# A routed layer's expert results added straight into the output's rows by accumulating DMAs, instead of through a table in DRAM

## The reference, cut to what matters

```python
xn = _layernorm(x, axis=-1)
x = x + gnn(xn, ...) + mix(xn)          # the long part ahead; x is now the residual
...
t = _layernorm(x)
logits = t @ switch_w + switch_b
route_prob_max = jnp.max(softmax(logits), axis=-1)
routes = jnp.argmax(softmax(logits), axis=-1)
for e in range(8):
    y = gelu(t @ w1[e] + b1[e]) @ w2[e] + b2[e]      # 1024 -> 512 -> 1024
    out = jnp.where((routes == e)[:, None], y, out)
out = out * route_prob_max[:, None]
return x + out
```

## Time and profile of the kernel before

| What | Value |
|---|---|
| median of three timed runs | 651.61 us (647.75 to 652.52) |
| the profiled execution's own time | 647.44 us |
| its span, first to last instruction | 645.6 us |
| busy share of the span: TensorE | 88% |
| VectorE | 72% |
| ScalarE | 49% |
| GpSimd | 33% |
| mean granted TensorE clock | 0.961 |
| bytes moved by DMA | 102.69 MB |

### The profile page before, as it was taken

How to read it: one execution, slowest core, us unless ns; L and a number is a source line. 1 busy time by engine, 2 the same in 40 slices (tenths; PEclk the granted TensorE clock), 3 DMA queues, 4 the chain that set the end, 5 groups by cost and what they waited for, 6 DMA issues and landing times.

```text
span 645.6 us, 9295 instructions
## 1 busy us (share of the span) xinstructions
PE 568.3 (88%) x3090; PEld 519.5 (80%) x3090; DVE 462.3 (72%) x800; ACT 318.2 (49%) x474; POOL 213.3 (33%) x183
## 2 busy tenths in 40 slices
PE   2799999999999999999898898999898769888850
PEld 2799997889999999998887788999786657767640
DVE  6688887867446444645798977887879655999962
ACT  3445553310333333532655654766553345998950
POOL 5566765765399000600079661000001100000001
PEclk9899999999999999999999998999999959999995
DMA  8365558530633433563221432222662212999935
GB/s 303 128 205 162 176 174 246 119 92 0 222 122 119 161 130 130 150 225 99 69 94 65 131 128 71 93 94 73 229 196 75 88 32 95 334 412 411 412 93 200
DMA packets 32962, 102.69 MB, mean 159 GB/s; under 512 B 5376, under 2 KB 9536, under 8 KB 32928
## 3 DMA queue, kind: packets, MB, share of 16 engines
q1 hardware_dynamic: 27792, 90.02, 41.2%
q0 software_dynamic: 4992, 11.72, 5.9%
q10 hardware_dynamic: 144, 0.52, 0.3%
HBM read 96.65 MB, written 5.60 MB: 158 GB/s over the span
## 4 chain that ended last, share of the span: by engine, by line
PE 59%; DVE 22%; issue 6%; DMA 6%; ACT 5%; POOL 1%; DVEq 0%; POOLq 0%; ACTq 0%; SPq 0%
PE ps L1473 35%; DVE wsp L910 6%; PE ps L1487 4%; DVE big L910 4%; PE ps L1652 3%; DMA raw<-in_w_experts 3%; PE ps L1596 2%; PE ps L1742 2%; PE ps L1581 2%; PE ps L1543 2%; PE ps L1524 2%; PE ps L1606 2%; DVE stats L927 1%; PE ps L1616 1%; ACT wsp L601 1%
## 5 line engine op out<-in xcount | busy, mean ns | idle before, releaser
L1473 PE MATMUL ps<-big,wsp 128*128 128x384 f32 x1680 | 305.1, 340 | 9.7 <-DVE wsp L910 6.0
L1473 PEld LDWEIGHTS ps<-big,wsp 128*128 128x128 f32 x1680 | 295.8, 191 | 14.3 <-DVE wsp L910 5.6
L910 DVE TENSOR_TENSOR wsp<-raw,wsp 128x1024 fp32r<-128x1024 f32 x117 | 153.7, 1325 | 29.1 <-ACT wsp L601 23.2
L601 ACT ACTIVATE wsp<-raw 128x1024 fp32r<-128x1024 f32 x83 | 87.2, 1052 | 33.1 <-PE ps L1487 12.9
L463 POOL TENSOR_SCALAR rs<-mv 128x1 f32<-128x1 f32 x12 | 7.8, 647 | 184.1 <-DVE mv L1212 119.6
L507 POOL DMA_INDIRECT edge_table<-ef,eidx x48 | 55.8, 1163 | 32.1 <-DMA edge_table<-ef,eidx 19.2
L608 ACT ACTIVATE big<-ps,bias 128x384 f32 x24 | 14.0, 582 | 81.1 <-PE ps L1473 81.1
L921 DVE SCALAR_TENSOR_TENSOR big<-ps,bias,big 128x384 f32 x24 | 14.8, 618 | 51.5 <-ACT big L608 49.5
L910 DVE TENSOR_TENSOR big<-raw_x,big 128x1024 fp32r<-128x1024 f32 x36 | 42.1, 1219 | 0.3 <-ACT big L773 0.3
L570 POOL DMA_DIRECT2D slot_y<-maskb x8 | 4.3, 542 | 109.3 <-DVE maskb L1390 109.3
L773 ACT ACTIVATE wsp<-raw 128x1024 fp32r<-128x1024 f32 x34 | 34.5, 1048 | 6.6 <-DMA raw<-in_w_experts 4.0
(11 more groups left out here) (245 smaller groups left out, 864.4 us busy)
## 6 DMA issues: line engine op xcount, KB each, us to landing
raw<-in_w_stream SPq DMA_DIRECT2D x85, 512.0 KB, 3.4
raw<-in_w_experts SPq DMA_DIRECT2D x32, 512.0 KB, 6.0
raw_x<-in_w_experts SPq DMA_DIRECT2D x32, 512.0 KB, 6.5
rowbuf<-in_rowb POOLq DMA_DIRECT2D x6, 512.0 KB, 6.3
raw_x<-in_w_stream SPq DMA_DIRECT2D x4, 512.0 KB, 7.0
slot_y<-maskb POOLq DMA_DIRECT2D x8, 256.0 KB, 5.7
tok<-in_x SPq DMA_DIRECT2D x3, 512.0 KB, 4.1
edges_a<-in_src_rows SPq DMA_DIRECT2D x8, 192.0 KB
```

The costliest lines, as they stand in the source:

```text
L601: nc.scalar.activation(wsp[:, 0, slot, :], raw[:, slot, :], ACT.Copy).then_inc(w_hi, 1)
L910: return nc.vector.tensor_tensor(dst, value, hi.bitcast(F32), ALU.subtract)
L1473: ins = nc.tensor.matmul(ps[:, bank, 0:N], wsp[:, a, slot, k * P:(k + 1) * P], moving[:, b, k, :], start=(k == 0 and n == 0), stop=(k == K ...
```

## The change

The table in DRAM is gone, with the early zeros for it, the gather at the end, VectorE's last three sums and SyncE's stores of the output. Instead:

- GpSimd stores the three tiles of residual rows `tok` to the output as soon as VectorE has added the projection, and waits for them (`rows_out`).
- TensorE gets, for each slot, the number of the output's row and the probability of each of its 64 tokens: the one-hot matrices of the slot times a small matrix `tag` (row number less 512, probability high, probability low), 24 matmuls of 4 columns, right after the first `up_bias` and ahead of `up` of expert 1. VectorE reads them from PSUM (`meta`) into `row_of` and `prob_of`. A place without a token gets the row number 512.
- ScalarE multiplies the high rows by the probability as it copies them (`half_of_y`), VectorE multiplies the low rows and adds (`rows_of_y`, now a scalar_tensor_tensor).
- GpSimd sends each slot's rows with one indirect DMA that adds them in DRAM to the output's rows (`compute_op=ALU.add`). Rows with a number over 383 are left out by the bounds check. VectorE's next `rows_of_y` waits for this DMA as it did for the store.
- The last slot is taken in two halves of 512 columns: a new semaphore `y_half` is set when the first bank is done.
- VectorE's ten steps for the tokens' rows (nine now, as the cast to `posi` is gone) move from ahead of `got_low` to the start of `routes`, behind it. `pos_done`, for which TensorE waits ahead of `up` of expert 1, moves with them.

```diff
@@ constants
+NO_ROW = 512.0
+META = 4
@@ GpSimd
             pool.wait_ge(bd_added, NT)
-            then(nc.gpsimd.memset(rowbuf[0:SLOT, 0, :], 0.0))
-            for s in range(EXPERTS, SLOTS):
-                pool.dma_start(ys_dram[s * SLOT:(s + 1) * SLOT, :], rowbuf[0:SLOT, 0, :]).then_inc(zero_out, 16)
-            pool.wait_ge(zero_out, 16 * OVER)
...
+            pool.wait_ge(wo_sum, 2 * NT)
+            for t in range(NT):
+                pool.dma_start(out[t * P:(t + 1) * P, :], tok[:, t, :]).then_inc(rows_out, 16)
+            pool.wait_ge(rows_out, 16 * NT)
+
+            def add_rows(s):
+
+                pool.wait_ge(meta_done, 1 if s < EXPERTS else s - EXPERTS + 2)
+                pool.wait_ge(y_sum, s + (1 if s < EXPERTS - 1 else 2))
+                pool.indirect_dma_start(
+                    out=out, out_offset=bass.IndirectOffsetOnAxis(ap=row_of[:, s:s + 1], axis=0),
+                    in_=y_buf, in_offset=None, bounds_check=N - 1, oob_is_err=False,
+                    compute_op=ALU.add).then_inc(y_out, 16)
+
             for s in range(EXPERTS):
-                pool.wait_ge(y_sum, s + 1)
-                pool.dma_start(ys_dram[s * SLOT:(s + 1) * SLOT, :], y_buf).then_inc(y_out, 16)
+                add_rows(s)
+            pool.wait_ge(y_out, 16 * EXPERTS)
             over = pool.value_load(rowi[0:1, OVER:OVER + 1], min_val=0, max_val=OVER)
...
-            for t in range(NT):
-                pool.indirect_dma_start(
-                    out=x2[t], out_offset=None, in_=ys_dram,
-                    in_offset=bass.IndirectOffsetOnAxis(ap=posi[:, t:t + 1], axis=0)).then_inc(yg_in[t], 16)
@@ ScalarE
-            def low_rows_of_y(e):
+            def half_of_y(e, s):
 
                 act.wait_ge(y_ready, ys.add())
                 if ys.n > 1:
-                    act.wait_ge(y_sum, ys.n - 1)
-                nc.scalar.activation(y_tmp, whole(4 + 2 * (e % 2))[SLOT:P, :], ACT.Copy).then_inc(y_low, 1)
+                    act.wait_ge(y_sum, ys.n - 1 if s < EXPERTS else ys.n)
+                nc.scalar.activation(y_tmp, whole(4 + 2 * (e % 2))[0:SLOT, :], ACT.Identity,
+                                     scale=prob_of[:, s:s + 1]).then_inc(y_low, 1)
+
+            def last_half_of_y(e):
+
+                act.wait_ge(y_sum, e)
+                for h, ready in ((0, (y_half, 1)), (1, (y_ready, ys.add()))):
+                    act.wait_ge(*ready)
+                    nc.scalar.activation(y_tmp[:, h * HALF:(h + 1) * HALF], ps[0:SLOT, 4 + 2 * (e % 2) + h, :],
+                                         ACT.Identity, scale=prob_of[:, e:e + 1]).then_inc(y_low, 1)
@@ VectorE, constants
+            nc.vector.memset(tag[:].bitcast(F32), 0.0)
+            for t in range(NT):
+                nc.vector.tensor_scalar(rt[:, R_POS, NT + t:NT + t + 1], cst[:, C_EXP:C_EXP + 1], t * P - NO_ROW, None,
+                                        ALU.add)
@@ VectorE, ahead of the gather
             dve.wait_ge(lexp_done, NT)
+            nc.vector.tensor_copy(tag[:, :, 0], rt[:, R_POS, NT:2 * NT])
             then(nc.vector.reciprocal(rt[:, R_PROB, 0:NT], rt[:, R_SUM, 0:NT]))
+            then(nc.vector.tensor_copy(tag[:, :, 1], rt[:, R_PROB, 0:NT]))
+            lo(tag[:, :, 2], rt[:, R_PROB, 0:NT], tag[:, :, 1]).then_inc(tag_done, 1)
@@ VectorE, slots
-            def rows_of_y(e):
-
-                dve.wait_ge(y_low, ys.add())
-                if ys.n > 1:
-                    dve.wait_ge(y_out, 16 * (ys.n - 1))
-                nc.vector.tensor_tensor(y_buf, whole(4 + 2 * (e % 2))[0:SLOT, :], y_tmp, ALU.add).then_inc(y_sum, 1)
+            def meta(first, n):
+
+                metas = ps[0:SLOT, meta_bank(first), 0:SLOTS * META].rearrange("p (s c) -> p s c", c=META)
+                dve.wait_ge(meta_ready, 1 if first == 0 else first - EXPERTS + 2)
+                nc.vector.tensor_scalar(row_of[:, first:first + n], metas[:, first:first + n, 0], NO_ROW, None, ALU.add)
+                nc.vector.reduce_sum(prob_of[:, first:first + n], metas[:, first:first + n, 1:3], AX_X)\
+                    .then_inc(meta_done, 1)
+
+            def rows_of_y(e, s):
+
+                dve.wait_ge(y_low, ys.add() if s < EXPERTS else s + 2)
+                if s:
+                    dve.wait_ge(y_out, 16 * s)
+                nc.vector.scalar_tensor_tensor(out=y_buf, in0=whole(4 + 2 * (e % 2))[SLOT:P, :],
+                                               scalar=prob_of[:, s:s + 1], in1=y_tmp,
+                                               op0=ALU.mult, op1=ALU.add).then_inc(y_sum, 1)
+
+            def last_rows(e):
+
+                dve.wait_ge(y_out, 16 * e)
+                for h in range(2):
+                    dve.wait_ge(y_low, ys.add())
+                    cols = slice(h * HALF, (h + 1) * HALF)
+                    nc.vector.scalar_tensor_tensor(out=y_buf[:, cols], in0=ps[SLOT:P, 4 + 2 * (e % 2) + h, :],
+                                                   scalar=prob_of[:, e:e + 1], in1=y_tmp[:, cols],
+                                                   op0=ALU.mult, op1=ALU.add).then_inc(y_sum, 1)
@@ TensorE
+            def meta(s, one_hot):
+
+                for t in range(NT):
+                    ins = nc.tensor.matmul(ps[0:SLOT, meta_bank(s), s * META:(s + 1) * META], one_hot(t),
+                                           tag[:, t, :], start=(t == 0), stop=(t == NT - 1))
+                return ins
...
             up_bias(0, 0)
+            pe.wait_ge(tag_done, 1)
+            for s in range(EXPERTS):
+                ins = meta(s, lambda t: place[t][:, s * SLOT:(s + 1) * SLOT])
+            ins.then_inc(meta_ready, 1)
             pe.wait_ge(pos_done, 1)
```

More of the change, by code:

```diff
@@ L573, in _ @@
                 for s in range(EXPERTS, SLOTS):
-                    pool.wait_ge(y_sum, s + 1)
-                    pool.dma_start(ys_dram[s * SLOT:(s + 1) * SLOT, :], y_buf).then_inc(y_out, 16)
-            pool.wait_ge(pos_done, 1)
-            pool.wait_ge(y_out, 16 * EXPERTS)
-            over = pool.value_load(rowi[0:1, OVER:OVER + 1], min_val=0, max_val=OVER)
-            with pool.If(over > 0):
+                    add_rows(s)
                 pool.wait_ge(y_out, 16 * SLOTS)
-            for t in range(NT):
-                pool.indirect_dma_start(
-                    out=x2[t], out_offset=None, in_=ys_dram,
-                    in_offset=bass.IndirectOffsetOnAxis(ap=posi[:, t:t + 1], axis=0)).then_inc(yg_in[t], 16)
         @block.scalar
@@ L1338, in _ @@
-            end = cum[:, 3, 4:12]
-            first = rt[:, R_FIRST, 0:EXPERTS]
             def every_token(a):
                 return a.unsqueeze(1).to_broadcast([P, NT, EXPERTS])
-            then(nc.vector.scalar_tensor_tensor(out=first, in0=cum[:, 3, 3:11], scalar=float(SLOT),
-                                                in1=rt[:, R_TOTAL, 0:EXPERTS], op0=ALU.mult, op1=ALU.add))
-            then(nc.vector.scalar_tensor_tensor(out=tile3(R_RANK), in0=cnt.rearrange("p (t e) -> p t e", t=NT),
-                                                scalar=float(SLOT), in1=every_token(first),
-                                                op0=ALU.is_ge, op1=ALU.mult))
@@ L1398, in _ @@
             prep_x()
+            meta(0, EXPERTS)
             hidden(0)
@@ L1440, in _ @@
                         prep_x()
-                    rows_of_y(0)
-            for t in range(NT):
-                dve.wait_ge(yg_in[t], 16)
-                nc.vector.scalar_tensor_tensor(out=tok[:, t, :], in0=x2[t], scalar=rt[:, R_PROB, t:t + 1],
-                                               in1=tok[:, t, :], op0=ALU.mult, op1=ALU.add).then_inc(sum_done, 1)
+                    meta(EXPERTS + o, 1)
+                    rows_of_y(0, EXPERTS + o)
         @block.tensor
@@ L1838, in _ @@
                     pe.wait_ge(got_lo, KT + o + 1)
+                    meta(EXPERTS + o, lambda t: place_late[:, t, :]).then_inc(meta_ready, 1)
                     up(0, 0, 0)
```

62 lines of the change are left out of this document (36 added, 26 removed).

## The result

The changed kernel takes **672.98 us** (median of 4 runs, 668.24 to 675.51), the kernel before 651.78 (4 runs, 647.75 to 652.52). The ratio is **1.034, with a 95% interval from 1.030 to 1.038**: 3.4% slower. The prediction said 642.6 us with a range of 634 to 655, so both its sign and its range were wrong. The profiled execution took 674.03 us with a span of 672.3, against a span of 645.6 before: 26.7 us to explain.

A forecast was written before the change was run, and what follows sets the result against it. TensorE and VectorE hold the chain, VectorE and DMA are full in the expert loop, and the tail is pure latency. Terms summed to -9.0 us, taken from the median 651.61 to give 642.6 us; range 634 to 655.

The forecast's parts named there:

- 9.0 us of room: Expert loop, slots 0 to 4: accumulating DMAs land in 7.3 to 8.9 us within 9.0 available, so VectorE's wait costs 0.
- slot 5: Before the sum of slot 6: slot 5's DMA takes 6.0 us where there are 5.6, +0.4 us.
- Rival 2: Every slot's sum waits for y_out because the DMA is slow in the full stream; 669 us at 12 us; chance 0.2.
- The tail: Kernel's end: 18.1 us behind the last sum's store issue become 5.0 for one accumulating DMA and 0.7 flag read, -12.4.
- The halves: Last slot taken in two halves: VectorE ends at 626.7 instead of 627.2, limited by slot 6's landing, -0.5 us.
- The stream: Full weight stream in the expert loop: an accumulated row costs two plain ones, +1.6 us, bounds -0.8 and +6.4.
- Rival 1: Accumulating DMA dear in the stream, a row costing four plain ones: stream term +6.4, total 651.9 us; chance 0.15.
- The start: Ahead of the expert loop: VectorE's constants +0.3, steps around the reciprocal +0.4, 24 small matmuls +1.2 us.
- The constants: Ahead of the loop: VectorE's one memset and three tensor_scalar of one column lengthen the chain, +0.3 us.
- the steps around the reciprocal: Ahead of the loop: three more steps of 0.1 to 0.2 us, with TensorE's gather waiting behind, +0.4 us.
- Hidden edits: Early tok stores, the zeros' removal and the slot sum's 1.28 for 1.22 us are covered by other work, 0.
- What would show it: Signs in the trace: end about 6 us after last issue, sums' period 11.1 us; landings over 9 us decide rival 2.

The follow-up runs named there:

- one SBUF input: The changed kernel with the 128x1024 subtractions of the experts' weights taking their second input from PSUM, so low parts are wrong: 650.17 us.
- two buffers: The changed kernel with a y_buf and semaphore each for even and odd slots: 648.63 us, ratio 0.999 to the kernel before.
- waits on SyncE: Even and odd slots with their own y_buf, plus SyncE instead of GpSimd waiting for the last landings: 644.1 us, ratio 0.991 to the kernel before.

## Why the prediction was wrong, step by step

- **The step that failed: "9.0 us of room ... the DMAs land in 7.3 to 8.9: just hidden, 0".** The transfer was estimated well; with the issue unhindered, the landings beside the full stream were 6.9 to 7.8 us (one SBUF input). What was wrong is the issue inside it. It was priced at 0.95 us by the earlier trace rows, where VectorE ran single instructions with gaps. Here it was 9.85 in four slots. The term was 0, and VectorE waited 7.26 + 6.95 + 7.32 + 4.91 = 26.4 us for the DMAs of slots 0, 2, 3 and 4. With slot 5's, which has a term of its own, these are the 29.8 us of waits and +28.4 of time. The trap is that the room of 9.0 us consists of just the work that holds the issue: a held one can't end before the room does.
- **The trace of before had a sign of it.** Its 48 scatters into the mask's table had issues from 0.95 to 1.91 us, half of them under 1.0, and I took one of the shortest. Of the longest, GpSimd's timeline of the kernel before:

```profile
73.00 0.96 POOL L507 DMA_INDIRECT edge_table<-ef,eidx  x1 [0.31 <-issue]
74.26 1.91 POOL L507 DMA_INDIRECT edge_table<-ef,eidx  x1 [0.30 <-issue]
...
79.86 1.71 POOL L507 DMA_INDIRECT edge_table<-ef,eidx  x1 [0.77 <-DVE eidx L991]
```

  and what VectorE did in that time:

```profile
74.12 1.23 DVE L910 TENSOR_TENSOR wsp<-raw,wsp 128x1024 fp32r<-128x1024 f32 x1 [0.39 <-ACT wsp L601]
75.26 0.56 DVE L910 TENSOR_TENSOR big<-work,big 128x384 f32 x1
...
79.51 1.21 DVE L910 TENSOR_TENSOR wsp<-raw,wsp 128x1024 fp32r<-128x1024 f32 x1
80.64 0.55 DVE L910 TENSOR_TENSOR big<-work,big 128x384 f32 x1
```

  Both long issues (74.26 to 76.17, 79.86 to 81.57) begin inside a short run of the very same subtraction and end 0.35 and 0.38 us behind it (75.82, 81.19), the first of them beside a next instruction that reads SBUF too. It wasn't so every time there either: an issue at 39.63, wholly beside such a subtraction, took 0.96. The question to ask was why issues of one line differ by a factor of two.
- **Rival 2 had the place, the price and the sign** (each slot's sum waits for `y_out`; at 12 us to the landing 669 us), with chance 0.2. Its reason, a slow DMA in a full stream, wasn't the cause: with the DMA engines' share cut to a third the held DMAs still took 13 us. It came to 673 with 15.6, 15.4, 15.8 and 13.4 us in the four held slots and 7.8 in slot 1.
- **The tail, -12.4, measured -6.7.** The last DMA was cheaper than its term (3.6 us where 5.0 was taken). The error is the drain of 6.5 us behind it, hidden before (to 644.67 of 645.6) and so in none of the rows I summed. It is the second failed step: "one accumulating DMA to its landing and the flag's read" left out what GpSimd itself still does. That is 5.7 us less than forecast. With two buffers, where no sum waits for `y_buf`, the whole gave 0 instead of -9.0, and the 5.7 are the largest part of that; moving the waits to SyncE brought 3.2 of them back.
- **The halves, -0.5, and slot 5, +0.4.** Both rest on a landing of 5.0 and 6.0 us. Slots 5 and 6 landed in 7.3 and 6.1, of which 4.17 and 3.04 were the issue, and VectorE waited 3.3 and 4.4 us for them. With short issues (one SBUF input) slots 5 and 6 landed in 4.6 and 4.5, and only the last half waited, 2.6.
- **The stream, +1.6, was right**: +1.1 with two buffers, where no sum waits for a DMA, and 618.24 - 562.51 - 53.92 = +1.8 with one SBUF input. Rival 1, with +6.4, is refuted.
- **The start, +1.9 in three terms, came to +3.1**, but not by these terms. 0.7 was there before the change begins (a step of VectorE at 473.20 for 472.50). The constants cost 0.2 (+0.3 forecast) and the steps around the reciprocal 0.3 (+0.4); 0.4 between the two is unexplained. The 24 small matmuls took 1.34 us in all, 545.70 to 547.07, and not 2.4: the lower bound was right, and from the first split to slot 0's sum it takes only 0.2 more than before. The nine moved steps ran with the other small ones from 544.28 to 547.73 without a gap, and the first split came at 547.73 instead of 544.80; but the copies ahead of them already ended 2.7 later (544.4 for 541.7), so that they added 0.3. The largest single part, 1.0, lies in TensorE's gather, whose matmuls are the same: from 525 to 535 us the granted clock was 0.56 where it was 0.75 before. Whether the change brought that about isn't shown. In the other kernels with this start it was 0.50 to 0.76, and slot 0's sum began from 558.69 (at 0.76) to 564.64 us (at 0.50).
- **Hidden edits** were hidden: the early stores of `tok` land in 5.6 us (median), 40 us ahead of the first slot's DMA; the slot's sum takes 1.28 for 1.22, as said.
- **What would show it** was chosen well. "Over 9 us makes it" was the right question to the trace, and the answer was 15.6.

## What to carry to other kernels

A duration is a price only for the company in which it was measured. An indirect DMA on GpSimd's queue cost 0.9 to 1.4 us of issue here beside an idle VectorE, and up to the whole length of a back-to-back run of VectorE instructions with two SBUF inputs. Before a DMA's landing becomes a wait of that same engine, look at what the engine does between the two. Here a second buffer took the wait away whole, a pause of VectorE only in part.

When the end of a kernel is shortened, list what every engine still does behind the old end's cover. Here GpSimd's 6.5 us came to light, and moving the last wait to another engine's queue was worth 3.2 us.

## What the runs showed of the hardware

- An issue of 9.85 us waits for the whole run of VectorE's two-input instructions, not for one of them: it ends 1.3 to 1.4 us after nine of them, or, with two buffers, within 0.1 us of the end of the 1.28 us sum that follows and has one tensor in SBUF. VectorE itself isn't slowed; two of its subtractions take 2.35 us with and without GpSimd waiting.
- It isn't a rule for every issue: beside the same burst some took 1.59 to 2.04 us. The set was the same in a repetition and another one in six altered kernels; what decides it is open.
- The add in an accumulating DMA of 4 KB rows cost 0.5 us of issue and 1.1 us to the landing when alone (1.40 and 3.6, against 0.89 and 2.5 us). With an unhindered issue it lands in 6.9 to 7.8 us beside a full stream.
- GpSimd ended each of these kernels with a drain. It took 6.52 us behind GpSimd's wait for the last landing and the flag's read, in the changed kernel and with two buffers; begun during the last issue it ended 6.5 us behind that issue (waits on SyncE). In the kernel before it ended 7.9 us behind the gather's last issue (644.67 for 636.80), so the 6.5 isn't a constant.
- Small matmuls with a weight tile of 64 columns and 4 moving columns took 1.34 / 24 = 0.056 us each, half of the 0.115 to 0.125 of those with 128 columns of weights and 8 or 64 moving ones.
